# First GNN layer: the masks of seven gathered edge columns made by seven per-column comparisons instead of one broadcast comparison

## The chip, the cores and the metric

The kernel runs on one core of a Trainium2 chip. The metric is the device time of one execution in microseconds; the kernel before has a median of 3071.47 us over three runs (3069.9 to 3072.8).

## The reference, cut to what matters

The inputs are a graph of 6250 nodes with 128 features and 200,000 edges, sorted by destination, with random sources. The first layer is a mean over incoming edges and a dense layer:

```python
neigh_sum = jax.ops.segment_sum(x[src], dst, num_segments=N)
deg = jax.ops.segment_sum(jnp.ones_like(src, dtype=x.dtype), dst, num_segments=N)
neigh_agg = jnp.where(deg[:, None] > 0, neigh_sum / jnp.maximum(deg, 1.0)[:, None], x)
h = jnp.concatenate([x, neigh_agg], axis=-1)
x = _layernorm(x + jax.nn.relu(h @ W.T + b), axis=-1)
```

The second layer is an edge-typed attention over the same edges (per-type key, query and value products, a softmax over the edges of a destination, a weighted sum of values), again with a residual and a layer norm. The change touches the first layer alone.

## The kernel before, in words

**The first layer** works through the edges in 49 steps (`sweep`, `i` from 0 to 48). A column is 128 edges, one on each partition. A step handles a period of 32 columns. 14 of them are gathered: POOL fetches the 128 source rows of each with an indirect DMA (line 669), in two runs of seven columns (`HALF = 7`), into three buffers `near` that take turns. Each node row in DRAM is 385 numbers of bf16: the features as three bf16 parts and a one for the degree. PE sums a run with seven matmuls of a 128x128 mask by 128x385 rows (`run_sum`, line 757). The other 18 columns are dense: PE picks their rows out of tables that stay in SBUF, by masks that DVE makes (`hot`, lines 1321 and 1322: for each column one comparison of a bf16 row of 128 and one of a bf16 row of 344, each with a key as a scalar of one fp32 number per partition). Of these, PE does a pick (line 723), ACT copies it (`take`, line 1078), and PE sums the slots (`slot_sum`, line 731, 49 of them in a step).

**The mask of a run** is made by `belong(i, h)` on DVE: `belongs[h][:, j, n]` is 1 where the key of the edge in column `j` is node place `n`. `belongs[0]` lies in the tile `ring`, `belongs[1]` is `more_belongs`. Before it writes, `belong` waits for the run two earlier to be summed (`runs_ps`). PE waits for `belongs_ready` at the places `h == 20` and `h == 46` of its own loop, ahead of the run it belongs to.

**The order within a step is written out by hand for each engine.** On DVE (`l0`, from line 1441) it is: in steps 4 to 12 one operation over all 1664 columns of edge digits (`digit_op`); join the slot sums of the step before; the last masks `hot` of group 2; `belong(i + 1, 0)`; add the node sums (`add_nodes`, line 1344); `by_types` (line 1409, four products whose result is the operand of PE's projections at line 804); `mean`; `hot` of groups 3 to 5; `copy_low` (line 1417, a copy out of PSUM of what PE made at line 820); `add_runs` (lines 1361 to 1368); `belong(i + 1, 1)`; `place_slots`; `stage_keys`; `hot`; `relu` with the layer norm's statistics (lines 1390 to 1394); `hot`; `normalise_x1`.

On ACT (`l0`, from line 1110) the 18 copies `take` go in order, and between copy 16 and copy 17 stands `deviation` (line 1091), the square root of the variance that DVE made at line 1394. Copy 17 therefore comes after it. PE's first `slot_sum` of the next step waits for copy 17 (`picked_ready`).

On PE (`l0`, from line 829) everything stands between the 49 `slot_sum`s at fixed places: `run_sum` at 2 and 23, `project_keys` (line 804) at 16, `low_keys` (line 820) at 27. `project_keys` waits for `by_types`.

On POOL there are the gathers, in order, and ahead of the fourth run the products of the edge-type weights (line 646). A gather of run `k` waits until run `k - 3` is summed.

**The second layer** runs after the whole first layer. Its 98 blocks gather 16 columns each from a table of keys and values (line 674).

Of the kernel before, what the change touches and what calls it, by code (L numbers as in the profile page):

```python
# [6 lines left out]
ALU = mybir.AluOpType  # L7
# [3 lines left out]
BF16 = mybir.dt.bfloat16  # L11
# [3 lines left out]
P = 128  # L15
# [7 lines left out]
HALF = 7  # L23
# [15 lines left out]
def gnn_kernel(nc, x, src, dst, etype, ntype, w0, b0, wq, wk, wv, we, mu, out):  # L39
# [53 lines left out]
    with ExitStack() as ctx:  # L93
        def sb(name, shape, dt=F32):
            return ctx.enter_context(nc.sbuf_tensor(name, shape, dt))

        def sem(name):
            return ctx.enter_context(nc.semaphore(name))
# [40 lines left out]
        gen_dst = sb("gen_dst", [P, 1])  # L139
        more_belongs = sb("more_belongs", [P, HALF * P // 2])  # L140
        run_sums = sb("run_sums", [P, D + 1])
        iota_g = sb("iota_g", [P, P])
        pick_cols = sb("pick_cols", [P, 3])
        inside = sb("inside", [P, CBLKS])
        far_s = sb("far_s", [P, 10])
# [63 lines left out]
        belongs = [t.bitcast(BF16).rearrange("p (j n) -> p j n", n=P) for t in (ring_part(HALF * P // 2), more_belongs[:, :])]  # L209
# [15 lines left out]
        col_keys = work[:, 0:2 * NAT].rearrange("p (a c) -> p a c", c=NAT)  # L225
# [98 lines left out]
        belongs_ready = sem("belongs_ready")  # L324
# [99 lines left out]
        def gathered_cols(i):  # L424
            return i * PERIOD
# [776 lines left out]
        def _(dve):  # L1202
# [144 lines left out]
            def belong(i, h):  # L1347

                k = 2 * i + h
                if k >= 2:  # L1350
                    dve.wait_ge(runs_ps, k - 1)
                first = gathered_cols(i) + h * HALF
                dve.tensor_tensor(belongs[h], col_keys[:, 1, first:first + HALF].unsqueeze(2).broadcast_to([P, HALF, P]),  # L1353
                                  iota_g[:, :].unsqueeze(1).broadcast_to([P, HALF, P]), ALU.is_equal).then_inc(belongs_ready, 1)

            def add_runs(i):

# [83 lines left out]
            def l0(i, late, early):  # L1441
# [4 lines left out]
                if i + 1 < ND:  # L1446
                    hot(i + 1, (i + 1) % 2, 2)
                    belong(i + 1, 0)
# [12 lines left out]
                if i + 1 < ND:  # L1461
                    belong(i + 1, 1)
# [14 lines left out]
            for h in range(2):  # L1477
                belong(0, h)
# [206 lines left out]
```

## Time and profile before

| what | value |
|---|---|
| median of three runs | 3071.47 us |
| the profiled execution | 3070.3 us, span 3068.2 us |
| mean granted TensorE clock | 0.883 |
| first layer, steady steps | 152 to 1014 us, 44 steps |
| length of a steady step | 19.34 to 19.37 us (from 394.56 us on) |
| length of a step with a digit operation | 20.25 to 21.12 us |
| second layer | after that to the end |
| busy over the span | PE 76%, DVE 50%, ACT 38%, POOL 73% |

An engine's busy time counts its own instructions; time in which it stands at a semaphore is idle. Where two instructions of an engine overlap in the records, the distance from the start of one to the start of the next is what one costs the queue, and it is shorter than the duration written beside it. The granted clock is 1.00 in the steady steps of the first layer. The steps were counted by the starts of line 1417, which DVE runs once in a step: 49 of them, at 152.01, 172.53 and so on to 1069.59 us. Between 152.01 and 1013.93 each of the 44 distances holds two instructions of line 1353.

### The profile page before, as it was taken

The page shows a single profiled execution, that of the slowest core. Times are in us where ns is not written, and L with a number is a line of the kernel's source. Part 1 is how long each engine was busy: PE and PEld are TensorE (multiplying, and loading weights), DVE is VectorE, ACT ScalarE, POOL GpSimd, SP SyncE. Part 2 cuts the span into 40 slices and gives each one's busy share as a digit, 9 for nine tenths or more (in the row PEclk, how much of TensorE's full clock was granted, in tenths as well). Part 3 has the DMA queues.
Part 4 walks back from the last instruction along what each step waited for, and adds up shares of the span by engine and source line. Part 5 has one row for each costly group of instructions (what it writes and reads, how often), then busy time and mean ns, then how long its engine had stood idle before and what let it go on. Part 6 is the DMA issues. An engine that isn't in the chain of part 4 may idle for free.

```text
span 3068.2 us, 37982 instructions
## 1 busy us (share of the span) xinstructions
PE 2340.0 (76%) x13394; PEld 1787.4 (58%) x13394; DVE 1531.3 (50%) x4631; ACT 1166.5 (38%) x2105; POOL 2245.9 (73%) x2302
## 2 busy tenths in 40 slices
PE   2799999999999756677766677767677767677766
PEld 1576777777777635555555555555555555555555
DVE  8788888888888513333333333333333333333334
ACT  5455555555555323323233223233223223222232
POOL 6877777777777177777777777777777777777774
PEclk8899999999999968888888888888888888888888
DMA  7254554444444333333333333333333333333332
GB/s 178 63 142 141 144 154 140 140 139 136 139 138 141 114 106 111 111 112 111 110 109 112 111 111 112 111 110 112 111 111 111 112 109 111 112 111 111 111 111 69
DMA packets 198686, 364.24 MB, mean 119 GB/s; under 512 B 61568, under 2 KB 130859, under 8 KB 192225
## 3 DMA queue, kind: packets, MB, share of 16 engines
q0 software_dynamic: 108112, 273.13, 32.6%
q1 hardware_dynamic: 88561, 87.77, 8.8%
q8 instruction: 107, 1.75, 0.2%
q10 hardware_dynamic: 1824, 0.92, 0.1%
q14 instruction: 82, 0.67, 0.1%
HBM read 294.37 MB, written 67.30 MB: 118 GB/s over the span
## 4 chain that ended last, share of the span: by engine, by line
POOL 50%; PE 18%; issue 18%; DVE 11%; ACT 1%; DMA 1%; SPq 0%; POOLq 0%; DVEq 0%
POOL ring L674 48%; PE banks L731 6%; PE banks L757 3%; PE banks L723 2%; PE banks L804 2%; DVE more_belongs L1353 1%; POOL ring L669 1%; PE banks L809 1%; PE banks L813 1%; DVE sums L1321 1%; PE banks L820 1%; DVE sums L1322 1%; DVE run_sums L1364 1%; POOL src_n L669 1%; PE banks L746 1%
## 5 line engine op out<-in xcount | busy, mean ns | idle before, releaser
L674 POOL DMA_INDIRECT ring<-kv_table,src_n x1563 | 1479.4, 946 | 476.3 <-issue 476.3
L965 PE MATMUL banks<-identf,ring 128*128 128x128 f32 x1568 | 294.5, 350 | 590.9 <-DMA ring<-kv_table,src_n 590.5
L1596 DVE COPY sums<-banks 128x512 f32<-128x512 f32 x392 | 260.6, 688 | 831.9 <-PE banks L980 830.1
L731 PE MATMUL banks<-sums,picks 128*126 128x385 bf16 x2401 | 587.0, 330 | 28.9 <-ACT picks L1078 20.3
L965 PEld LDWEIGHTS banks<-identf,ring 128*128 128x128 f32 x1568 | 242.6, 182 | 615.3 <-DMA ring<-kv_table,src_n 612.4
L669 POOL DMA_INDIRECT ring<-x_part_rows,work x462 | 479.6, 1038 | 154.2 <-issue 134.3
L1078 ACT ACTIVATE picks<-banks 128x343 bf16<-128x343 f32 x882 | 437.8, 512 | 323.1 <-PE banks L723 296.9
L1162 ACT ACTIVATE work<-banks,negmax 128x2048 f32<-128x2048 f32 x98 | 192.9, 1968 | 791.5 <-DVE negmax L1547 785.6
L1170 ACT ACTIVATE work<-banks 128x512 f32<-128x512 f32 x392 | 221.7, 593 | 592.8 <-PE banks L965 592.8
L1544 DVE TENSOR_REDUCE largest<-banks 128x1 f32<-128x2048 f32 x98 | 224.6, 2292 | 363.9 <-PE banks L950 363.9
L731 PEld LDWEIGHTS banks<-sums,picks 128*126 128x126 bf16 x2401 | 316.0, 136 | 144.5 <-ACT picks L1078 38.4
L987 PEld LDWEIGHTS banks<-ring,sums 128*128 128x128 f32 x3136 | 365.5, 192 | 47.8 <-issue 46.4
L987 PE MATMUL banks<-ring,sums 128*128 128x128 f32 x3136 | 366.1, 275 | 1.1 <-DVE sums L1596 1.1
L950 PE MATMUL banks<-work,queries 128*128 128x512 f32 x784 | 365.6, 609 | 0.0
L980 PE MATMUL banks<-identf,work 128*128 128x128 f32 x1568 | 307.9, 379 | 1.1 <-ACT work L1162 1.1
L980 PEld LDWEIGHTS banks<-identf,work 128*128 128x128 f32 x1568 | 299.4, 209 | 2.2 <-ACT work L1162 1.3
L1322 DVE TENSOR_SCALAR sums<-iota_k,keys_g 128x344 bf16<-128x344 bf16 x882 | 291.2, 330 | 0.0
L669 POOL DMA_INDIRECT src_n<-x_part_rows,work x224 | 234.2, 1046 | 73.7 <-issue 64.6
L723 PE MATMUL banks<-sums 128*128 128x343 bf16 x882 | 275.4, 313 | 2.7 <-ACT picks L1078 1.6
L1321 DVE TENSOR_SCALAR sums<-iota_n,keys_g 128x128 bf16<-128x128 bf16 x882 | 242.9, 275 | 43.3 <-PE banks L723 40.9
L950 PEld LDWEIGHTS banks<-work,queries 128*128 128x128 f32 x784 | 141.9, 191 | 184.3 <-issue 184.3
L723 PEld LDWEIGHTS banks<-sums 128*128 128x128 bf16 x882 | 87.1, 99 | 42.5 <-issue 14.6
(257 smaller groups left out, 2158.5 us busy)
## 6 DMA issues: line engine op xcount, KB each, us to landing
kv_table<-ring SPq DMA_DIRECT2D x49, 1024.0 KB, 4.6
ring<-kv_table,src_n POOLq DMA_INDIRECT x1563, 2.8
ring<-x_part_rows,work POOLq DMA_INDIRECT x462
x_part_rows<-sums SPq DMA_DIRECT2D x7, 675.5 KB, 7.6
src_n<-x_part_rows,work POOLq DMA_INDIRECT x224
sums<-x_rows SPq DMA_DIRECT2D x51, 64.0 KB, 2.1
x_rows<-ring SPq DMA_DIRECT2D x49, 64.0 KB
queries_t<-q_tile SPq DMA_DIRECT2D x49, 64.0 KB
```

What stands on the lines that cost most here:

```text
L669: pool.indirect_dma_start(near[k % RUNS][:, j, :], None, part_dram, bass.IndirectOffsetOnAxis(ap=col_ids[:, first + j:first + j + 1], axis ...
L674: pool.indirect_dma_start(kv_ring[u][:, j, :], None, table, bass.IndirectOffsetOnAxis(ap=of, axis=0)).then_inc(l1_rows[2 * u + j // RUN], 16)
L723: pe.matmul(bank[c % 2][:, 0:KEYS], hot_low[:, c % HOT_RING, :], hot_key[:, c % HOT_RING, 0:KEYS], start=True, stop=True).then_inc(pick_ps, 1)
L731: mm = pe.matmul(bank[2 + i % 2][0:SLOTS, 0:3 * D + 1], picked[:, i % 2, h, 0:SLOTS], x_parts[:, h, 0:3 * D + 1], start=(h == 0), stop=(h ...
L950: mm = pe.matmul(bank[g], queries[:, :], keysT[:, g, :], start=False, stop=True, skip_group_check=True)
L965: tr = pe.transpose(bank[KEY_BANK[g]][:, j * P:(j + 1) * P], kv_ring[k.u][:, g * 4 + j, 0:D], identf[:, :])
L980: tr = pe.transpose(bank[PROB_BANK[g]][:, j * P:(j + 1) * P], probT[:, at:at + P], identf[:, :])
L987: mm = pe.matmul(bank[7][:, 0:D], prob[:, j, :], kv_ring[k.u][:, j, D:2 * D], start=(j == 0), stop=(j == COLS - 1))
L1078: act.activation(picked[:, par, :, c * NW:(c + 1) * NW], bank[c % 2][:, 0:KEYS].rearrange("p (h w) -> p h w", w=NW), ACT.Copy).then_inc(pi ...
L1321: dve.tensor_scalar(hot_low[:, c % HOT_RING, :], iota_n[:, :], keys_g[:, par, 1, c:c + 1], None, ALU.is_equal)
L1322: ins = dve.tensor_scalar(hot_key[:, c % HOT_RING, :], iota_k[:, :], keys_g[:, par, 0, c:c + 1], None, ALU.is_equal)
L1596: dve.tensor_copy(prob[:, g * 4:(g + 1) * 4, :].rearrange("p a b -> p (a b)"), bank[PROB_BANK[g]]).then_inc(prob_copied, 1)
```

## The change

One comparison of 128x896 elements is replaced by seven of 128x128. Before, both inputs are fp32 and lie in SBUF: the seven keys of the run, each broadcast over 128 places, and the row of places broadcast over the seven columns. After, the row of places is the only tensor that is read, now as bf16, and the key of the column is a scalar operand, one fp32 number per partition. The output (bf16, 0 or 1) is the same. The semaphore is raised by the last of the seven. `HALF` is 7, so each `belong` issues seven instructions where it issued one; there are 98 calls of it. `iota_g` is 256 bytes a partition where it was 512.

```diff
-        iota_g = sb("iota_g", [P, P])
+        iota_g = sb("iota_g", [P, P], BF16)
...
                 first = gathered_cols(i) + h * HALF
-                dve.tensor_tensor(belongs[h], col_keys[:, 1, first:first + HALF].unsqueeze(2).broadcast_to([P, HALF, P]),
-                                  iota_g[:, :].unsqueeze(1).broadcast_to([P, HALF, P]), ALU.is_equal).then_inc(belongs_ready, 1)
+                for j in range(HALF):
+                    ins = dve.tensor_scalar(belongs[h][:, j, :], iota_g[:, :], col_keys[:, 1, first + j:first + j + 1], None,
+                                            ALU.is_equal)
+                ins.then_inc(belongs_ready, 1)
```

## Rows read from the trace of the kernel before

**Rows 1.** Window of one steady step: busy us (instructions) of PE, PEld, DVE, ACT, POOL; granted clock; DMA share; GB/s.
```profile
588.11:607.47 19.36, 18.95 (x122) 14.30 (x121) 16.22 (x66) 11.34 (x25) 14.72 (x14) 1.00 0.49 140
```

**Rows 2.** Chain that ended last, that step: start us, us, what.
```profile
593.99 0.19 DVE aggr L1394
...
594.20 0.29 ACT rstd L1091
```

**Rows 3.** Timeline of PE, same step: start, us, line, operation, [idle before].
```profile
594.94 0.54 PE L731 MATMUL banks<-sums,picks 128*126 128x385 bf16 x2 [0.41 <-ACT picks L1078]
...
600.09 1.16 PE L804 MATMUL banks<-work,ring 128*128 128x128 f32 x8
601.09 0.33 PE L731 MATMUL banks<-sums,picks 128*126 128x385 bf16 x1
...
601.56 1.05 PE L809 MATMUL banks<-ring,work 128*128 128x128 f32 x8
602.45 0.49 PE L731 MATMUL banks<-sums,picks 128*126 128x385 bf16 x2
```

**Rows 4.** Timeline of DVE, same step, columns as in rows 3.
```profile
588.11 0.69 DVE L1417 COPY ring<-banks 128x512 f32<-128x512 f32 x1 [1.71 <-PE banks L820]
...
590.33 1.09 DVE L1353 TENSOR_TENSOR more_belongs<-work,iota_g 128x896 bf16<-128x896 f32 x1
591.33 0.35 DVE L1337 TENSOR_SCALAR sums<-iota_s,slot_node 126x256 f32<-126x256 f32 x1
...
594.44 0.36 DVE L1321 TENSOR_SCALAR sums<-iota_n,keys_g 128x128 bf16<-128x128 bf16 x1
594.61 0.30 DVE L1322 TENSOR_SCALAR sums<-iota_k,keys_g 128x344 bf16<-128x344 bf16 x1
594.82 0.25 DVE L1321 TENSOR_SCALAR sums<-iota_n,keys_g 128x128 bf16<-128x128 bf16 x1
...
597.43 0.49 DVE L1322 TENSOR_SCALAR sums<-iota_k,keys_g 128x344 bf16<-128x344 bf16 x1
597.84 1.07 DVE L1353 TENSOR_TENSOR ring<-work,iota_g 128x896 bf16<-128x896 f32 x1
598.84 0.41 DVE L1344 TENSOR_TENSOR ring<-ring,banks 128x258 f32<-128x258 f32 x1
599.17 0.87 DVE L1409 SCALAR_TENSOR_TENSOR work<-work,banks 128x128 f32<-128x128 int32 x4
599.96 0.14 DVE L1379 TENSOR_SCALAR deg<-ring 128x1 f32<-128x1 f32 x1
600.03 0.14 DVE L1380 TENSOR_SCALAR deg<-ring 128x1 f32<-128x1 f32 x1
...
601.92 0.43 DVE L1322 TENSOR_SCALAR sums<-iota_k,keys_g 128x344 bf16<-128x344 bf16 x1
602.27 0.24 DVE L1321 TENSOR_SCALAR sums<-iota_n,keys_g 128x128 bf16<-128x128 bf16 x1
```

**Rows 5.** Timeline of POOL, same step.
```profile
596.90 0.94 POOL L669 DMA_INDIRECT ring<-x_part_rows,work  x1 [0.80 <-PE banks L757]
598.15 1.58 POOL L669 DMA_INDIRECT ring<-x_part_rows,work  x1 [0.30 <-issue]
```

**Rows 6.** Timeline of DVE, the step from 192.85 us.
```profile
192.85 0.69 DVE L1417 COPY ring<-banks 128x512 f32<-128x512 f32 x1 [1.74 <-PE banks L820]
...
200.40 1.02 DVE L1428 TENSOR_SCALAR spare_n<-dst_n 128x1664 int32<-128x1664 int32 x1
...
213.17 0.69 DVE L1417 COPY ring<-banks 128x512 f32<-128x512 f32 x1 [1.74 <-PE banks L820]
```

**Rows 7.** Chain that ended last, start of the layer.
```profile
66.43 2.10 POOL ring L669
...
141.70 1.62 POOL ring L669
...
155.04 5.43 DMA src_n<-x_part_rows,work
```

## The prediction

> **What bounds the kernel now.** The change lies in the first layer, so I read that stage before anything else. The busy shares of the whole span (DVE 50%, POOL 73%) say nothing about it: they are averages over two layers with different limits. The window of one steady step [rows 1] says more. PE is busy 18.95 of 19.36 us at full clock, DVE 16.22, ACT 11.34. POOL shows 14.72, and it has a gap of 0.30 us ahead of each gather besides (14 of them, 4.2 us), which makes 18.9. So PE is the limit, all but 0.41 us, and the question is what that 0.41 us waits for, because a longer DVE step would show there first.
>
> The chain of waits names it [rows 2]. DVE finishes the variance of the tile at 593.99 + 0.19 = 594.18, and ACT starts its square root at 594.20. The last of ACT's 18 copies stands behind it, and PE's first slot sum, at 594.94, has been idle for 0.41 us until that copy [rows 3]. This is place A. The DVE work ahead of it began with the copy of line 1417 at 588.11, which itself had waited 1.71 us for PE [rows 4]. So PE releases DVE, DVE releases ACT, and ACT releases PE: the idle DVE time lies before the chain and can't absorb anything put inside it. The mask of run 1, `more_belongs` at 590.33, is inside.
>
> There is a second place, which the chain doesn't name. `by_types` on DVE ends at 599.17 + 0.87 = 600.04 [rows 4], and PE's line 804, which reads its result, starts at 600.09 [rows 3]. Its eight matmuls take 601.09 - 600.09 = 1.00 us to the next instruction, where the same eight of line 809 take 602.45 - 601.56 = 0.89. So PE stands there too, for 0.11 us and some start-up: place B. The same 0.05 or 0.06 us lies between the two in 40 of the 44 steps. From 588.11 to 600.04 DVE has no gap, and both masks of the step lie in that stretch. A step in which DVE has one more operation shows how such a stretch passes delay on: the operation of line 1428, 1.02 us, stands between A and B, and the step from 192.85 to 213.17 takes 20.32 us, 0.96 more than 19.36 [rows 1, 6]. A microsecond of DVE ahead of B is almost a microsecond of the step.
>
> **The change, part by part.** *What is removed.* A broadcast comparison costs DVE's queue the distance to the next start: 591.33 - 590.33 = 1.00 us for one mask, 598.84 - 597.84 = 1.00 for the other [rows 4].
>
> *What is added.* Seven comparisons of 128 bf16 places with an fp32 scalar. The trace has exactly this form: line 1321. It costs 594.61 - 594.44 = 0.17 us to the next start [rows 4]; the other pairs of a step show 0.16 or 0.17, and I take 0.165. Line 1322, the same with 344 places, costs 594.82 - 594.61 = 0.21 to 0.22. The 216 places more cost 0.05 us, so 128 cost about 0.03 and the other 0.13 is per instruction. Seven make 7 x 0.165 = 1.155. Each mask grows by 0.155, the two of a step by 0.31 (with 0.16 and 0.17 for one: 0.24 to 0.38). Splitting one instruction into seven pays the fixed part six times more, and that is more than the faster streaming returns.
>
> *Meeting POOL.* In the trains of lines 1321 and 1322 some instructions are stretched when a gather ends: the one at 601.92 takes until 602.27, 0.35 where 0.22 is usual, and the one at 597.43 takes 0.41 until 597.84 [rows 4], which is when the gather of 596.90 ends (596.90 + 0.94) [rows 5]. So short scalar comparisons are held up for 0.13 to 0.19 us about once per gather, which come every 1.25 us, and a train of 1.16 us would meet 0.9 of them. The broadcast comparison behaves otherwise: the gather beside it takes 1.58 us in place of 0.94 [rows 5], so it holds POOL off. A new cost is therefore up to 2 x 0.19 = 0.38 us a step. Against it, the hold-up ahead of the second mask (0.19) may fall elsewhere. Bounds: -0.19 to +0.38. POOL's place in the step will shift and the present stretches may only move, so nothing favours one end, and I take the middle, +0.09.
>
> The Trainium skill ("SBUF — State Buffer", Who interferes with whom) says that an instruction in a two-port mode and a GpSimd one exclude each other, whoever starts first, and that a comparison with two SBUF inputs takes only the read side, so that descriptor generation should pass. By this rule the broadcast form would not have stretched a gather; the rows disagree, 1.58 against 0.94. By the rule the new form would also meet POOL where the old one did not, and the sum would be that of the upper bound.
>
> *On the path.* Per step 0.31 + 0.09 = 0.40 us, between 0.24 - 0.19 = +0.05 and 0.38 + 0.38 = +0.76. At A the delay of the first mask, some 0.2, adds to the idle 0.41 one for one. At B PE arrives late by that much, but DVE is late by both masks, so PE waits for the rest. The step grows by the full 0.40. There are 44 distances between starts of line 1417 from 152.01 to 1013.93 us with two masks each, so 44 x 0.40 = 17.6 us (2 to 33). The last step, with one mask, adds 0.2 at most, which I leave out.
>
> *The start of the layer.* Until 155.04 us the chain runs through POOL's gathers, and PE's run waits for the last one's data [rows 7]. DVE idles there, so its longer masks are hidden; but POOL instructions stand longer beside a broadcast comparison: the first is the gather at 66.43, 2.10 us in place of 0.94 (1.15 lost), the last the one at 141.70, 1.62 us (0.67 lost), and with three between them (two gathers, one product of the weights) these five lose 3.5 us. Short comparisons let POOL in between; beside lines 1321 and 1322 gathers take 0.94 to 1.0. I take 3.0 back, between 0 and 3.5.
>
> *Free of cost.* In the steady steps the freed POOL time (0.6 us a mask) is worth nothing: POOL already waits for PE, 0.80 us before the gather at 596.90 of which 0.30 is its usual gap [rows 5]. PE asks for `belongs_ready` late: each mask is made some half a step or more before the place (`h == 20` or `h == 46` of PE's next pass) where PE wants it. The smaller `iota_g` moves addresses only. The second layer has none of this.
>
> *Sum.* 17.6 - 3.0 = +14.6 us on the profiled 3070.3 (span 3068.2, 2.1 around it). The median is 1.2 above that run; 3071.5 + 14.6 = 3086.
>
> **Rivals.** *Hidden:* DVE has 3.1 us idle in a step, and if the chain had slack that I don't see, or if POOL's hold-ups mostly vanish, the step grows by at most 0.1: 4.4 - 3.0, so 3073. For it: the chain view doesn't pass through the mask of 597.84. Against it: the 0.05 us at B and the step with the digit operation. Chance 0.15.
>
> *Faster:* the seven run closer together than line 1321 does. The cheapest small scalar operation of the trace, line 1379 with one column, costs 600.03 - 599.96 = 0.07 us to the next [rows 4]. With 0.03 for streaming, seven cost 0.70, and each mask is 0.3 us cheaper. PE's idle time is then what can be won: 0.3 at A, the 0.11 at B, so 0.41 x 44 = 18, with the start 21: 3050. It turns in its favour below 1.00 / 7 = 0.143 us per comparison. Against it: line 1379 has an immediate as its scalar and line 1321 a tensor, and 0.16 is the least usual value of line 1321. Chance 0.06. The Trainium skill ("Vector Engine (DVE) Microarchitecture Reference", Measured stream behaviour on trn2) puts about 75 ns on each instruction after queue overlap; an estimate by it is 0.76 us for seven, 0.24 less a mask, and a time of some 3053. This case's line 1321 disagrees, with 0.13 per instruction.
>
> *Worse:* each train is held up by POOL in full: 0.76 a step, 44 x 0.76 = 33 us with nothing won at the start, 3105. For it, the new trains offer POOL seven openings. Chance 0.09.
>
> **How the numbers follow.** Forecast (both places bind, 0.2 to 0.6 us a step): 0.70. Its own range is 44 x 0.2 - 3 = +6 to 44 x 0.6 - 2 = +24, so 3077 to 3096. With the rivals, 8 in 10 lies in 3074 to 3097. A measurement of this kernel tells from no change about 0.2%, 6.1 us. Slower than 3077.6: the forecast nearly whole and the worse case, 0.79; within: 0.15; faster: 0.06.
>
> **What would show it.** Line 1321's form under the changed line at 0.16 to 0.17 us from start to start, seven to 1.15 to 1.3 us; steady steps of 19.6 to 20.0 us; PE's idle time before the first slot sum of 0.5 to 0.7; line 804 still 0.05 us behind line 1409, with PE idle before it; no gather near 1.58 us beside a mask; and PE's first run fed 2 to 3.5 us earlier. The prediction is wrong if the seven take under 1.00 us together, or if line 804 stops following line 1409.

## The result, and the profile after

The changed kernel takes 3076.81 us, median of 18 runs (3075.05 to 3078.57), against 3069.86 for the kernel before in the same series (18 runs, 3068.08 to 3073.76). The ratio is 1.0021 with a 95% interval of 1.0014 to 1.0028: 6.5 us slower by the ratio and 6.95 between the medians, where 14.6 were forecast. The sign was right; the sum was more than twice too large. The profiled execution after took 3075.05 us with a span of 3072.9 and stands 4.75 above the one profiled before. One execution of `h0_only` below took 7733.83 us where its nine others took 3071 to 3076; no profile shows why, and its ratio leaves it out.

The window of one steady step, which answers to [rows 1]:

```profile
590.17:609.75 19.58, 19.07 (x122) 14.22 (x121) 16.47 (x77) 11.36 (x25) 13.42 (x15) 1.00 0.49 139
```

A step is 19.58 us where it was 19.36. PE's busy time hardly moves (19.07 against 18.95); POOL's falls from 14.72 to 13.42. The timeline of DVE in that step, which answers to [rows 4]:

```profile
590.17 0.69 DVE L1419 COPY ring<-banks 128x512 f32<-128x512 f32 x1 [1.70 <-PE banks L820]
...
592.38 1.23 DVE L1354 TENSOR_SCALAR more_belongs<-iota_g,work 128x128 bf16<-128x128 bf16 x7
593.52 0.35 DVE L1337 TENSOR_SCALAR sums<-iota_s,slot_node 126x256 f32<-126x256 f32 x1
...
594.01 0.26 DVE L1321 TENSOR_SCALAR sums<-iota_n,keys_g 128x128 bf16<-128x128 bf16 x1
594.18 0.30 DVE L1322 TENSOR_SCALAR sums<-iota_k,keys_g 128x344 bf16<-128x344 bf16 x1
594.40 0.33 DVE L1321 TENSOR_SCALAR sums<-iota_n,keys_g 128x128 bf16<-128x128 bf16 x1
...
599.58 0.49 DVE L1322 TENSOR_SCALAR sums<-iota_k,keys_g 128x344 bf16<-128x344 bf16 x1
599.99 1.31 DVE L1354 TENSOR_SCALAR ring<-iota_g,work 128x128 bf16<-128x128 bf16 x7
601.12 0.41 DVE L1344 TENSOR_TENSOR ring<-ring,banks 128x258 f32<-128x258 f32 x1
601.46 0.87 DVE L1411 SCALAR_TENSOR_TENSOR work<-work,banks 128x128 f32<-128x128 int32 x4
...
609.75 0.69 DVE L1419 COPY ring<-banks 128x512 f32<-128x512 f32 x1 [1.70 <-PE banks L820]
```

The first mask takes 593.52 - 592.38 = 1.14 us of DVE's queue, the second 601.12 - 599.99 = 1.13, each 0.13 to 0.14 more than the one comparison. The masks of lines 1321 and 1322 behind the first one run on at 0.16 to 0.22 us from start to start, without the hold-up of 0.06 that stood there before, where line 1322 took 592.26 - 591.98 = 0.28:

```profile
591.98 0.37 DVE L1322 TENSOR_SCALAR sums<-iota_k,keys_g 128x344 bf16<-128x344 bf16 x1
592.26 0.23 DVE L1321 TENSOR_SCALAR sums<-iota_n,keys_g 128x128 bf16<-128x128 bf16 x1
```

Before the second mask, line 1322 at 599.58 still takes 0.41 us to the next start. From the copy at 590.17 to the end of `by_types` it is 601.46 + 0.87 - 590.17 = 12.16 us, and it was 11.93. The timeline of PE, which answers to [rows 3]:

```profile
597.09 0.54 PE L731 MATMUL banks<-sums,picks 128*126 128x385 bf16 x2 [0.51 <-ACT picks L1078]
...
602.38 1.16 PE L804 MATMUL banks<-work,ring 128*128 128x128 f32 x8
603.37 0.33 PE L731 MATMUL banks<-sums,picks 128*126 128x385 bf16 x1
```

Place A is idle for 0.51 us (0.41 before). Line 804 starts at 602.38, 0.05 behind the end of `by_types`, as before, and takes 603.37 - 602.38 = 0.99 us. From the first slot sum to line 804 it is 602.38 - 597.09 = 5.29 us, and it was 5.15: the step grew by about 0.10 at A and 0.14 between A and line 804. Both places moved the way the prediction had them. POOL, which answers to [rows 5]:

```profile
592.49 0.96 POOL L669 DMA_INDIRECT ring<-x_part_rows,work  x1 [0.30 <-issue]
...
599.06 0.94 POOL L669 DMA_INDIRECT ring<-x_part_rows,work  x1 [1.74 <-PE banks L757]
600.31 0.94 POOL L669 DMA_INDIRECT ring<-x_part_rows,work  x1 [0.30 <-issue]
```

The gather at 592.49 ends at 593.45, inside the first train of seven, and the train takes no longer for it. The gather at 600.31 lies beside the second mask and takes 0.94 us; none stands near 1.58 any more, and the wait ahead of the gather at 599.06 has grown from 0.80 to 1.74. The start of the layer, in PE's timeline: the run whose data PE waited for at the end of the chain in [rows 7]:

```profile
157.45 1.33 PE L757 MATMUL banks<-src_n,ring 128*128 128x385 bf16 x7 [0.68 <-DMA src_n<-x_part_rows,work]
```

It came at 160.51 before, after 1.14 us of waiting. The first copy of line 1419 (1417 before) starts at 149.29 instead of 152.01: 2.7 us earlier. The 44th distance later it stands at 1021.07 instead of 1013.93, so the 44 steps took 871.78 us where they took 861.92: 9.86 more, 0.22 each. 9.86 - 2.72 = 7.14, close to the 6.95 between the medians. (The second layer was 2.3 us shorter in the profiled execution after; its code is the same, and the medians don't show it.)

### The profile page after: what moved, and what is told of

Its sections match the earlier page's. It is cut to its first block, busy times and chain, and to the rows that moved or that the text cites. A ratio compares the mean times of both kernels' runs of the same rounds, so it can differ in the third digit from the quotient of the medians.

```text
span 3072.9 us, 38570 instructions
## 1 busy us (share of the span) xinstructions
PE 2343.7 (76%) x13394; PEld 1783.7 (58%) x13394; DVE 1542.9 (50%) x5219; ACT 1167.4 (38%) x2105; POOL 2191.9 (71%) x2302
## 4 chain that ended last, share of the span: by engine, by line
POOL 50%; PE 21%; issue 17%; DVE 10%; ACT 1%; DMA 1%; POOLq 0%; SPq 0%; DVEq 0%
POOL ring L674 48%; PE banks L731 7%; PE banks L757 3%; PE banks L723 2%; PE banks L804 2%; DVE more_belongs L1354 2%; PE banks L809 1%; PE banks L813 1%; POOL ring L669 1%; PE banks L820 1%; DVE sums L1321 1%; DVE sums L1322 1%; PE banks L823 1%; POOL src_n L669 1%; PE banks L746 1%
## 5 line engine op out<-in xcount | busy, mean ns | idle before, releaser
L669 POOL DMA_INDIRECT ring<-x_part_rows,work x462 | 445.4, 964 | 195.0 <-issue 125.3
L669 POOL DMA_INDIRECT src_n<-x_part_rows,work x224 | 216.3, 965 | 92.1 <-issue 60.3
L1321 DVE TENSOR_SCALAR sums<-iota_n,keys_g 128x128 bf16<-128x128 bf16 x882 | 232.2, 263 | 42.0 <-PE banks L723 39.7
L723 PEld LDWEIGHTS banks<-sums 128*128 128x128 bf16 x882 | 88.7, 101 | 42.4 <-issue 14.6
```

The lines of the kernel that those rows point to most:

```text
L669: pool.indirect_dma_start(near[k % RUNS][:, j, :], None, part_dram, bass.IndirectOffsetOnAxis(ap=col_ids[:, first + j:first + j + 1], axis ...
L723: pe.matmul(bank[c % 2][:, 0:KEYS], hot_low[:, c % HOT_RING, :], hot_key[:, c % HOT_RING, 0:KEYS], start=True, stop=True).then_inc(pick_ps, 1)
L1321: dve.tensor_scalar(hot_low[:, c % HOT_RING, :], iota_n[:, :], keys_g[:, par, 1, c:c + 1], None, ALU.is_equal)
```

## The experiments

Theory: a step costs what lies on DVE between the copy of line 1417 and line 804, one for one. The rivals: only the chain through ACT's square root counts; the elements or the meeting with POOL set the cost; DVE's total or POOL is the limit. The step lengths below are means over the 29 distances from the fifteenth on; the kernel before has 19.36, the changed one 19.59 (19.60 in `changed_3`, a second profile of it; in both, two of the steps take 19.72 or 19.73 and the others 19.57 to 19.59).

**One mask at a time.** Both rows of places are kept, the fp32 one and a bf16 one, and one of the two masks of a step has the new form.

```diff
+                if h == 0:
+                    for j in range(HALF):
+                        ins = dve.tensor_scalar(belongs[h][:, j, :], iota_gb[:, :], ...)
+                    ins.then_inc(belongs_ready, 1)
+                else:
+                    dve.tensor_tensor(belongs[h], ...)
```

> The mask of the first run of a step (the one written into the tile ring, between places A and B) is made by seven comparisons, the other by the one broadcast comparison of before. Theory (DVE's queue time ahead of line 804 is what a step costs, one for one): the mask grows by 0.13 to 0.14 us, the step from 19.36 to 19.49 or 19.50, while PE's idle time at its first slot sum stays at 0.41. Rival (only what stands on the chain through ACT's square root counts): the step stays at 19.36.

`h0_only`: 19.49 us a step (19.48 to 19.50), as the theory has it. It took 3074.63 us, ratio 1.0013 (1.0003 to 1.0023). Its PE timeline:

```profile
616.99 0.54 PE L732 MATMUL banks<-sums,picks 128*126 128x385 bf16 x2 [0.41 <-ACT picks L1079]
...
621.14 0.72 PE L732 MATMUL banks<-sums,picks 128*126 128x385 bf16 x3
621.70 0.31 PE L724 MATMUL banks<-sums 128*128 128x343 bf16 x1
621.85 0.49 PE L732 MATMUL banks<-sums,picks 128*126 128x385 bf16 x2
622.28 1.16 PE L805 MATMUL banks<-work,ring 128*128 128x128 f32 x8
```

Place A is untouched at 0.41, and yet the step is 0.13 longer: the cost lies behind A. Half of it shows at the slot sums of 621.14 (621.70 - 621.14 = 0.56 us, 0.49 before), half ahead of line 804 (in this kernel 805), which follows the slot sums of 621.85 after 0.43 us (0.36 before). The stretch of DVE that ends with line 804's operand is what both wait for, and the chain of waits named neither. The rival that counts only the chain through the square root falls.

> The mask of the second run (more_belongs, ahead of place A) is made by seven comparisons, the other by the one broadcast comparison. Theory: the mask grows by 0.14 and the comparisons behind it lose a hold-up of 0.06, so the step goes from 19.36 to 19.44, and PE's idle time at its first slot sum from 0.41 to 0.49. Rival (only the chain through ACT's square root counts): the whole 0.23 us that the change added to a step is here, 19.58.

`h1_only`: 19.71 us a step on average, between 19.62 and 19.79, and 3080.85 us, ratio 1.0034 (1.0021 to 1.0046). Half of the change costs more than all of it: its six times, 3079.57 to 3084.40, all lie above the 3078.57 that the changed kernel took at most. Theory (19.44, and 0.49 at A) and rival (19.58) both missed; A is idle for 0.77 us on average. The profiled execution is the slowest of the six, 3.55 us above their median, so by an estimate (3.55 / 44) the steps of the others are 0.08 shorter, which is still more than the changed kernel's. Its DVE timeline behind the mask, and the gather beside it:

```profile
615.18 1.42 DVE L1357 TENSOR_SCALAR more_belongs<-iota_gb,work 128x128 bf16<-128x128 bf16 x7
616.32 0.41 DVE L1339 TENSOR_SCALAR sums<-iota_s,slot_node 126x256 f32<-126x256 f32 x1
...
617.41 0.49 DVE L1324 TENSOR_SCALAR sums<-iota_k,keys_g 128x344 bf16<-128x344 bf16 x1
617.82 0.24 DVE L1323 TENSOR_SCALAR sums<-iota_n,keys_g 128x128 bf16<-128x128 bf16 x1
```

```profile
616.88 0.95 POOL L670 DMA_INDIRECT src_n<-x_part_rows,work  x1 [0.30 <-issue]
```

The mask itself is again 616.32 - 615.18 = 1.14. But line 1324 at 617.41 takes 0.41 us until 617.82, where 0.22 is usual, and 617.83 is just when the gather ends (616.88 + 0.95). It is a hold-up of 0.19 that the changed kernel doesn't have at this place, and line 1339 at 616.32 has another, 0.33 in place of 0.27. POOL runs in another phase here: its gathers start 0.12, 1.37, 2.62 us after the copy, in the changed kernel 1.07, 2.32, 3.59. One broadcast comparison a step still holds it off, which may be why; no run tests that.

**The fixed part and the elements.** In `eight_pieces` the first column is compared in two halves:

```diff
-                for j in range(HALF):
+                for lo, hi in ((0, 64), (64, P)):
+                    dve.tensor_scalar(belongs[h][:, 0, lo:hi], iota_g[:, lo:hi], col_keys[:, 1, first:first + 1], None,
+                                      ALU.is_equal)
+                for j in range(1, HALF):
...
```

> As the changed kernel, but the first of the seven columns is compared in two halves of 64 places: eight instructions with the same number of elements. Theory (0.13 us per instruction, whatever its length, and one for one into the step): each mask 0.13 longer, 1.27 us, the step 19.58 + 0.26 = 19.84. Rival (the cost is the elements or the meeting with POOL's gathers, not the number of instructions): the step stays within 0.05 of 19.58.

19.84 us a step, as expected to the hundredth. One execution took 3090.05 us.

```profile
617.88 0.39 DVE L1354 TENSOR_SCALAR more_belongs<-iota_g,work 128x64 bf16<-128x64 bf16 x2
618.18 1.06 DVE L1357 TENSOR_SCALAR more_belongs<-iota_g,work 128x128 bf16<-128x128 bf16 x6
619.15 0.35 DVE L1337 TENSOR_SCALAR sums<-iota_s,slot_node 126x256 f32<-126x256 f32 x1
```

The two halves cost 0.30 us, the other six 0.97, which is 0.16 each: one more instruction with no more elements is 0.13 to 0.14.

`seven_fp32` is the changed kernel without `BF16` in the line of `iota_g`.

> As the changed kernel, but the row of places stays fp32: seven comparisons of 128 fp32 places. Theory: 0.13 us per instruction plus 128 fp32 places at half the rate of bf16, so 0.20 from start to start, 1.39 us a mask, the step 19.58 + 0.5 = 20.1. Rival (what the type of the row does is hidden by the fixed part): 1.14 us a mask and 19.58.

1.37 us a mask (0.196 an instruction), 20.09 us a step (20.03 to 20.15), 3099.26 us in one execution: as expected. `row_only` is the reverse, the kernel before with the row of places in bf16.

> The kernel before with the row of places in bf16 and nothing else: one broadcast comparison with one fp32 and one bf16 input. Theory: no faster mode with one fp32 input, 1.00 us a mask, step 19.36, time of before within 0.1%. Rival (the type of the row alone changes the comparison's rate or its meeting with POOL): another mask time or another step.

The mask keeps 1.00 us to the next start and 1.09 of duration, so the type of the row gives one broadcast comparison nothing. Its time, 3597.25 us, can't be used: in that series the kernel before itself took 3587 us, with steps of uneven length.

**Masks taken out of the stretch, or made shorter inside it.** `moved_seven_3` and `moved_one_3` are the changed kernel and the kernel before with both masks ahead of the copy:

```diff
                     hot(i + 1, (i + 1) % 2, 2)
-                    belong(i + 1, 0)
...
+                if i + 1 < ND:
+                    belong(i + 1, 0)
+                    belong(i + 1, 1)
                 if late:
                     copy_low(late)
                 add_runs(i)
-                if i + 1 < ND:
-                    belong(i + 1, 1)
```

Both, and a third kernel that is shown below, were first run in two series in which the kernel before itself took 3587 and 3584 us. They gave 3721, 3611 and 3689 us, then 3719, 3620 and 3702: all slower than the kernel before. Nothing on record says why 3070 became 3585 there. It wasn't the chip as such: the second of these series and the one below, with 3070, carry the same chip number. The six runs are left out of the argument; their expectations were:

> As the changed kernel, but both masks of the next step are made just ahead of the copy of line 1417, after the last picks' masks, where DVE stood idle for 0.9 and 1.7 us waiting for PE. Theory (the masks cost only as they lie between that copy and line 804): neither place A nor B binds any more, PE loses no 0.41 + 0.11 us in a step, the steady step is 18.85 us, steps with a digit operation are under 19.6, and the whole is 25 to 33 us under before: 3037 to 3045. Rival (DVE's total work per step limits, or POOL does): a step at or above 19.36.

> As the kernel before, one broadcast comparison a mask, with the masks moved in the same way. Theory: the same 18.85 us a step, since the length of the masks no longer matters; each mask still holds POOL off by 0.6, so a step of POOL is 14 x 1.25 + 1.1 = 18.6, just under. The start of the layer is 2.7 us later than with seven comparisons: 3040 to 3049. Rival: POOL becomes the limit and the step is 18.9 to 19.2.

> Masks at their old places, made by one comparison with both inputs bf16: the keys of the run copied beforehand into eight adjacent bf16 numbers, the row of places laid out eight times, the mask stored with the seven columns adjacent, so that PE reads each column's mask with a stride of 16 bytes. If two elements a cycle are reached, a mask takes 1024 / 2 / 0.96 GHz + 0.07 = 0.60 us and the copy of the next keys 0.1 to 0.2, so 0.75 against 1.00. Theory: each step gets back up to 0.5 us of PE's idle time, 18.9 to 19.1 a step, unless PE's weight loads with a stride are slower. Rival (the masks' time is not what a step costs): 19.36.

> The kernel of moved_seven again, since the chip of that series ran the kernel before itself in 3587 us, with steps of uneven length. Seven comparisons a mask, both masks just ahead of the copy of line 1417, where DVE waited for PE. Theory (the masks cost only as they lie between that copy and line 804): neither place A nor B binds, the steady step is 18.85 us, steps with a digit operation are under 19.6, the whole 3037 to 3045. Rival (DVE's total work per step limits, or POOL does): a step at or above 19.36.

> The kernel of moved_one again: one broadcast comparison a mask, the masks moved in the same way. Theory: the same 18.85 us a step, the length of the masks no longer matters; POOL, held off by 1.1 us a step, needs 18.6 and is just under. The start of the layer is 2.7 us later than with seven comparisons: 3040 to 3049. Rival: POOL becomes the limit, 18.9 to 19.2 a step.

> The kernel of packed_bf16 again: masks at their old places by one comparison with both inputs bf16. In the series on the slow chip the mask took 0.61 us and the copy of the next keys 0.08. Theory: 0.69 in place of 1.00 a mask, so the chain up to line 804 is 0.6 us shorter, up to A 0.3; PE's idle time goes from 0.41 + 0.11 to 0.1 and 0: 18.9 to 19.0 a step, 3040 to 3052, unless PE's weight loads with a stride of 16 bytes are slower. Rival (the masks' time is not what a step costs): 19.36.

The runs that count, with the changed kernel beside them:

> The changed kernel itself, beside the next three on one chip. Theory: steady steps of 19.58 us and 0.2% above the kernel before. Rival: none; it is the yardstick.

> Seven comparisons a mask, both masks just ahead of the copy of line 1417, where DVE waited for PE. Theory (the masks cost only as they lie between that copy and line 804): neither place A nor B binds, the steady step is 18.85 us on a chip that runs the kernel before in 3070, steps with a digit operation are under 19.6, the whole 3037 to 3045. Rival (DVE's total work per step limits, or POOL does): a step at or above 19.36. Second rival, from the two series in which the kernel before took some 3585 us: a kernel that keeps PE busier is slowed by more, on every chip.

> One broadcast comparison a mask, the masks moved in the same way. Theory: 18.85 us a step, 3040 to 3049. Rival: POOL, held off by the broadcast comparisons, becomes the limit, 18.9 to 19.2 a step.

`packed_bf16_3` leaves the masks where they are and makes each with one comparison of 16-bit operands:

```diff
-                    mm = pe.matmul(bank[4][:, 0:3 * D + 1], belongs[h][:, j, :], near[k % RUNS][:, j, 0:3 * D + 1],
+                    mm = pe.matmul(bank[4][:, 0:3 * D + 1], belongs[h][:, :, j], near[k % RUNS][:, j, 0:3 * D + 1],
...
+            def stage_run(k):
+                first = gathered_cols(k // 2) + k % 2 * HALF
+                dve.tensor_copy(run_keys[:, k % 2, :], col_keys[:, 1, first:first + 8]).then_inc(run_vec, 1)
...
+                dve.tensor_tensor(belongs[h], run_keys[:, h, :].unsqueeze(1).broadcast_to([P, P, 8]), iota_g,
+                                  ALU.is_equal).then_inc(belongs_ready, 1)
...
```

> Masks at their old places by one comparison with both inputs bf16, 0.61 us, and 0.08 for the copy of the next keys. Theory: 18.9 to 19.0 us a step, 3040 to 3052, unless PE's weight loads with a stride of 16 bytes are slower. Rival (the masks' time is not what a step costs): 19.36.

| kernel | us | ratio to before, 95% | step, us |
|---|---|---|---|
| changed_3 | 3076.44 | 1.0023 (1.0012 to 1.0033) | 19.60 |
| moved_seven_3 | 3054.62 | 0.9952 (0.9935 to 0.9968) | 19.21 |
| moved_one_3 | 3057.71 | 0.9961 (0.9947 to 0.9975) | 19.18 |
| packed_bf16_3 | 3058.20 | 0.9961 (0.9947 to 0.9975) | 19.19 |

All three beat both kernels, so the masks' place and length in the stretch are what counts, and once out of it the two forms have the same step within 0.03 us. The steps of `moved_seven_3` are uneven, 18.92 to 19.52 us; the other two keep within 0.07. The packed mask on DVE:

```profile
621.72 0.69 DVE L1359 TENSOR_TENSOR more_belongs<-run_keys,ring 128x1024 bf16<-128x1024 bf16 x1
622.33 0.17 DVE L1351 CAST run_keys<-work 128x8 bf16<-128x8 f32 x1
...
629.21 0.67 DVE L1359 TENSOR_TENSOR ring<-run_keys,ring 128x1024 bf16<-128x1024 bf16 x1
629.80 0.16 DVE L1351 CAST run_keys<-work 128x8 bf16<-128x8 f32 x1
```

0.61 us and 0.07 for the next keys, where it was 1.00. But all three stop at 19.2, and not at 18.85 (the masks moved) or 18.9 to 19.0 (the packed mask), and all three times lie above what was expected. For `moved_one_3` 19.18 is also what the rival with POOL as the limit had; `root_last_moved_one` below decides against it. The chain that ended last in `moved_seven_3` says why:

```profile
601.19 0.24 PE banks L784 x2
...
601.46 0.30 DVE ring L1392
...
602.44 0.19 DVE aggr L1396
...
602.65 0.29 ACT rstd L1091
602.95 0.39 ACT picks L1078
...
603.38 0.54 PE banks L731 x2
```

DVE's first operation of the statistics now starts 0.03 us behind PE's line 784. From there the way is PE, DVE, square root, last copy, slot sum, and PE stands for 0.38 us whatever the masks do (0.38 also in `packed_bf16_3` and `moved_one_3`; in `moved_seven_3` 0.38 in this step and 0.41 on average). Of the 0.41 idle at A before, only 0.03 was the masks'. Line 804 no longer waits:

```profile
627.68 1.05 PE L804 MATMUL banks<-work,ring 128*128 128x128 f32 x8
628.57 0.33 PE L731 MATMUL banks<-sums,picks 128*126 128x385 bf16 x1
```

It takes 0.89 us in place of 1.00, and with the two slot sums ahead of it 1.22 in place of 1.36. So the gain was 0.03 at A + 0.14 at line 804, and not 0.5.

**The square root behind the last copy.** One number, on three kernels:

```diff
-                    if early and c == 16:
+                    if early and c == 17:
                         deviation(early)
```

> The changed kernel with ACT's square root behind its last copy instead of ahead of it, so that PE's first slot sum no longer waits for DVE's variance. Theory (the step is the stretch from the copy of line 1417 to line 804 plus a fixed rest of PE; place A only shares in the waiting): PE's idle time at A goes, the same time is idle at B, and the step stays at 19.58. Rival (the two idle times of PE add up, each with a gain of its own): 19.1.

> moved_seven_3, whose step stopped at about 19.18 us with 0.38 idle at A, with ACT's square root behind its last copy. Theory (what is left at A is PE's own line 784, its statistics on DVE, the square root and the last copy, in a row): the idle time goes, 18.8 to 18.9 a step, 44 x 0.3 = 14 us under moved_seven_3: 3038 to 3044. Rival (DVE or POOL is the limit at 19.18): no change.

> The same with one broadcast comparison a mask. POOL has no wait for PE left in moved_one_3, a gather beside two broadcast comparisons takes 2.25 us, and its step is 19.17. Theory: POOL is at its limit there, so the step stays between 19.0 and 19.2 and seven comparisons, which let POOL in, are now worth 0.2 to 0.3 us a step. Rival (POOL has room that the trace does not show): 18.8 to 18.9 as with seven.

`root_last_changed`: 19.58 us a step, 3075.60 us, ratio 1.0019 (1.0010 to 1.0029).

```profile
620.64 0.49 PE L731 MATMUL banks<-sums,picks 128*126 128x385 bf16 x2
621.38 0.38 PE L731 MATMUL banks<-sums,picks 128*126 128x385 bf16 x1 [0.25 <-DVE ring L1344]
...
622.17 1.16 PE L804 MATMUL banks<-work,ring 128*128 128x128 f32 x8
```

The idle time at A is gone (the profile shows no wait for ACT there), and it turns up ahead of line 804 instead, most of it at the slot sum that waits for line 1344: 621.38 - 620.64 = 0.74 us for two slot sums that take 0.33 elsewhere. The step is what was expected, and the rival's 19.1 falls. While the stretch to line 804 sets the step, place A is worth nothing.

`root_last_moved_seven`: 18.91 us a step, 3045.26 us, ratio 0.9923 (0.9910 to 0.9937), the fastest of all, and 1.3 us above the 3038 to 3044 that were expected: 9.4 under `moved_seven_3` where 14 were expected. `root_last_moved_one`: 18.91 too, 3049.48 us, ratio 0.9936 (0.9921 to 0.9951). The expectation that POOL would hold this one at 19.0 or more is wrong, although POOL never waits for PE in it:

```profile
633.76 2.08 POOL L669 DMA_INDIRECT ring<-x_part_rows,work  x1 [0.30 <-issue]
```

The gather that meets the two broadcast comparisons (632.93 to 635.02) takes 2.08 us and ends 0.82 after them, and POOL still keeps up. What seven comparisons are worth there is mostly the start of the layer: the first copy stands at 148.84 us against 151.96, the length of the 44 steps is 841.2 and 842.3, and the medians differ by 4.2 us.

## Why the prediction was half right

**The two places, and one for one: right.** The distance of 0.05 or 0.06 us between `by_types` and line 804 is the same in every kernel whose masks in the stretch take 1.00 us or more; with the packed mask it is 0.34, and with the masks moved 0.36, and there line 804 no longer waits. `h0_only` shows that the second mask costs its full 0.13 without touching A, `root_last_changed` that A may vanish without a gain, and `eight_pieces` and `seven_fp32` that 0.26 and 0.5 more on DVE are 0.25 and 0.5 more in a step.

**The price of seven: nearly.** 0.13 us for each instruction and 0.03 for 128 places held (`eight_pieces`, `seven_fp32`). The sum used 0.165 for one and 1.155 for seven; measured were 1.14 and 1.13. The term "0.31 a step" is 0.27.

**The meeting with POOL: the step that failed.** The sum added 0.09 a step, "the middle of the bounds" of -0.19 to +0.38, for a train of short comparisons that "would meet 0.9 of them", each time with a hold-up of up to 0.19. It was -0.04: 12.16 - 11.93 = 0.23 of stretch, less the 0.27 of the masks. Neither train was held up, though a gather ended inside the first (at 593.45); a hold-up of 0.06 behind the first mask went (before, line 1322 at 591.98 us took 0.28 to the next start), and the one of 0.19 before the second stayed. The number of short instructions doesn't set the hold-ups: `h1_only` has 0.12 more a step than the whole change with half of it. The phase between POOL and DVE fits better: each stretched instruction ends where a gather ends. In the kernel before and in the changed one the steps are alike (19.35 to 19.37; 19.57 to 19.59 but for two), so there is one outcome and no mean, and a middle of bounds is just a guess; in `h1_only` and `moved_seven_3` it isn't as regular. That the phase is the cause is argued and not shown: no run here shifted the phase and nothing else.

**The sum.** 44 x 0.40 = 17.6 became 9.9, so 9.9 - 2.7 = 7 in place of 14.6. Of the 7.7 us that the steps fell short, 44 x 0.04 = 1.8 is the price of seven and 44 x 0.13 = 5.7 the meeting with POOL. The measured 3076.81 lies inside 3074 to 3097, but just under the 3077 to 3096 of the forecast's own case: a step grew by 0.22 to 0.23, near the lower end of its 0.2 to 0.6. It also lies under 3077.6, up to which the prediction counted an outcome as no change; the 18 runs of each kernel, with an interval of 1.0014 to 1.0028, tell it from none.

**The start: right.** 3.0 us were to come back there and 2.7 did. In `h0_only` the same 2.7 us were there at the first copy and lost in the next step (22.86 us); in the changed kernel that step is 20.56. PE waited there for a gather, and the run behind it was slow:

```profile
158.51 2.38 PE L758 MATMUL banks<-src_n,ring 128*128 128x385 bf16 x7 [1.82 <-DMA src_n<-x_part_rows,work]
```

The same seven matmuls take 1.33 us in the changed kernel, after a wait of 0.68. The granted clock between 158.5 and 161 us is 0.52 in `h0_only`, and 1.00 between 157.4 and 161 in the changed kernel.

**What hid nothing.** DVE is idle for 3 us in a step, and that did not help, since it all lies on the other side of the copy: the masks put there cost nothing in either form. The rival "faster" was also priced wrongly. It counted 0.3 of the 0.41 us at A as something to be won, but a shorter chain wins 0.03: the packed mask is 0.3 us shorter and gained 0.17 a step in all.

## What to carry to other kernels

Splitting one long vector instruction into several short ones pays the fixed part each time; compare the distance from start to start of the same form in the trace with the long one divided by their number before counting elements. Find every place where the bound engine stands, also those that the chain of waits doesn't name: an instruction that starts 0.05 us after its operand is ready, step for step, is one. Idle time at a place is what could be won only if the next latest arrival there is known; and work with a late consumer belongs where its engine waits, whatever its form.

## What the runs showed of the hardware

- A `tensor_scalar` with a per-partition scalar costs DVE's queue 0.13 us beside its elements; 0.03 more for 128 bf16 places, 0.07 for 128 fp32 ones (0.163 and 0.196 from start to start).
- A two-input comparison with both inputs bf16 and the last dimension with step one takes 0.61 us for 1024 elements, although one input repeats along the middle dimension. With one fp32 input (`row_only`), as with two, it takes 1.00 for 896.
- The gather that is stretched by broadcast comparisons ends 0.82 us after the last of them (598.15 + 1.58 against 597.84 + 1.07; 633.76 + 2.08 against 635.02). In the steady steps it takes 1.33 to 1.81 us beside one, by when it started, 1.16 to 1.37 beside the shorter packed one, and 2.07 to 2.29 beside two; gathers beside seven short bf16 comparisons take 0.94 to 1.09. The Trainium skill ("SBUF — State Buffer", Who interferes with whom) infers that a comparison with two SBUF inputs leaves descriptor generation alone, and says that it contends with a GpSimd instruction that reads SBUF. The gather here reads its row numbers out of SBUF (the tile `work`) and is stretched; so the rule that the prediction took from this section may simply not cover it, and no run here tells the two apart.
- PE's loads of a 128x128 bf16 mask took 144 ns with a stride of 16 bytes (`packed_bf16_3`) and 97 without, and the matmuls behind them 328 and 326: the slower load was hidden.
